# Expert weights of a mixture-of-experts kernel: loads on ScalarE's DMA queue, down pieces split behind the tile loop

## The reference

```python
def _moe_forward(hidden_states, gate_weight, w_gate, w_up, w_down):
    ...
    topk_w, topk_idx = jax.lax.top_k(scores, K)          # K = 8 of E = 64
    topk_w = topk_w / jnp.sum(topk_w, axis=-1, keepdims=True)
    ...
    sorted_tokens = expanded[order]
    group_sizes = jnp.zeros((E,), jnp.int32).at[flat_ids].add(1)
    g = jax.lax.ragged_dot(sorted_tokens, w_gate, group_sizes)
    u = jax.lax.ragged_dot(sorted_tokens, w_up, group_sizes)
    out = jax.lax.ragged_dot(jax.nn.silu(g) * u, w_down, group_sizes)
    ...
    y = jnp.sum(outs * topk_w[:, :, None], axis=1)
x = x + _L0_xattn_ref(_layernorm(x, axis=-1), ctx_2048, ...)
x = x + _L0_ffn_ref(_layernorm(x, axis=-1), ...)
```

## Time and profile before

| | |
|---|---|
| median of 3 runs | 7184.59 us (7184.37 to 7189.35) |
| span of the profiled execution (the page gives its span alone) | 7176.6 us |
| PE busy | 6780.5 us, 94% of the span |
| DVE, ACT, POOL busy | 46%, 42%, 16% |
| experts stage, first gate matmul to last tile's | 3040.19 to 7142.80 us |
| largest part of the chain that ended last, beside PE | DMA 12%, of it `moe_rec_s<-table` 9% |
| bytes moved | 1047.60 MB, mean 146 GB/s |

### The profile page before, as it was taken

The page is one execution under the profiler, slowest core; times in us unless marked ns, Lnnn a source line. Parts: engine busy times, 40 slices in busy tenths (PEclk is TensorE's granted clock), DMA queues, the critical chain, the costliest instruction groups (busy, mean ns, idle before and its releaser), DMA issues.

```text
span 7176.6 us, 104484 instructions
## 1 busy us (share of the span) xinstructions
PE 6780.5 (94%) x34594; PEld 5983.0 (83%) x34595; DVE 3268.1 (46%) x4163; ACT 2987.2 (42%) x3554; POOL 1143.4 (16%) x1037
## 2 busy tenths in 40 slices
PE   8989899999999699699999999999999999999998
PEld 6778787888888577588989888999899999988987
DVE  3433323999999588632343333332322223323333
ACT  3321223888888444333343343332422333333333
POOL 0000000000000145411111111111111111111111
PEclk9999999999999899799999999999999999999999
DMA  7663455555555587555565565554644555555555
GB/s 224 191 199 132 160 137 117 125 130 131 129 125 130 144 159 155 122 146 148 152 199 150 154 174 152 154 152 102 173 103 102 128 129 152 130 148 152 143 144 141
DMA packets 691794, 1047.60 MB, mean 146 GB/s; under 512 B 260259, under 2 KB 489636, under 8 KB 691718
## 3 DMA queue, kind: packets, MB, share of 16 engines
q1 hardware_dynamic: 578916, 672.36, 32.1%
q0 software_dynamic: 112656, 374.28, 23.5%
q10 hardware_dynamic: 146, 0.00, 0.0%
HBM read 724.14 MB, written 322.31 MB: 146 GB/s over the span
## 4 chain that ended last, share of the span: by engine, by line
PE 34%; DMA 12%; ACT 6%; issue 3%; DVE 1%; SPq 1%; ACTq 0%; DVEq 0%; POOLq 0%
DMA moe_rec_s<-table 9%; PE moe_ps_y L1249 4%; PE moe_ps_y L1251 4%; PE moe_ps_y L1250 4%; PE moe_ps_gate L1262 3%; PE moe_ps_gate L1263 3%; PE moe_ps_gate L1264 3%; DMA out<-moe_y,moe_rec_s 3%; PE moe_ps_up L1264 3%; PE moe_ps_up L1262 3%; PE moe_ps_up L1263 3%; ACT moe_gu_hi L1291 2%; ACT moe_d_hi L1291 2%; PE moe_ps_xT L1239 2%; DVE moe_d_lo L1336 1%
## 5 line engine op out<-in xcount | busy, mean ns | idle before, releaser
L1300 ACT ACTIVATE moe_y<-moe_ps_y,moe_rec_s 128x1024 f32<-128x1024 f32 x287 | 320.4, 1116 | 1633.1 <-DMA moe_rec_s<-table 1331.2
L1351 DVE TENSOR_TENSOR moe_hT_lo<-moe_ps_hT,moe_hT_hi 128x384 fp32r<-128x384 f32 x286 | 159.4, 557 | 1637.3 <-ACT moe_hT_hi L1312 1637.3
L1262 PE MATMUL moe_ps_gate<-moe_gu_hi,moe_xT_hi 128*128 128x384 f32 x2288 | 797.7, 349 | 43.1 <-DVE moe_gu_lo L1336 28.0
L1249 PE MATMUL moe_ps_y<-moe_d_hi,moe_hT_hi 128*128 128x512 f32 x1722 | 711.8, 413 | 89.2 <-DVE moe_hT_lo L1351 89.2
L1219 POOL DMA_INDIRECT out<-moe_y,moe_rec_s x287 | 457.7, 1595 | 2083.6 <-ACT moe_y L1300 1987.5
L1263 PE MATMUL moe_ps_gate<-moe_gu_lo,moe_xT_hi 128*128 128x384 f32 x2288 | 772.5, 338 | 0.0
L1264 PE MATMUL moe_ps_gate<-moe_gu_hi,moe_xT_lo 128*128 128x384 f32 x2288 | 772.0, 337 | 0.0
L1264 PE MATMUL moe_ps_up<-moe_gu_hi,moe_xT_lo 128*128 128x384 f32 x2288 | 765.1, 334 | 0.0
L1262 PE MATMUL moe_ps_up<-moe_gu_hi,moe_xT_hi 128*128 128x384 f32 x2288 | 764.2, 334 | 0.0
L1263 PE MATMUL moe_ps_up<-moe_gu_lo,moe_xT_hi 128*128 128x384 f32 x2288 | 764.2, 334 | 0.0
L1251 PE MATMUL moe_ps_y<-moe_d_hi,moe_hT_lo 128*128 128x512 f32 x1722 | 685.9, 398 | 0.0
(11 more groups left out here) (223 smaller groups left out, 14061.0 us busy)
## 6 DMA issues: line engine op xcount, KB each, us to landing
moe_raw_g<-in_w_gate SPq DMA_DIRECT2D x64, 1536.0 KB, 9.0
moe_raw_u<-in_w_up SPq DMA_DIRECT2D x64, 1536.0 KB, 11.0
moe_raw_d<-in_w_down SPq DMA_DIRECT2D x64, 1536.0 KB, 11.5
vst<-proj_v_o SPq DMA_DIRECT2D x64, 512.0 KB, 2.6
att_kt<-kst SPq DMA_DIRECT2D x64, 512.0 KB, 3.5
att_qh<-qst SPq DMA_DIRECT2D x128, 256.0 KB, 4.7
att_ql<-qst SPq DMA_DIRECT2D x128, 256.0 KB, 5.5
att_v<-vst SPq DMA_DIRECT2D x128, 256.0 KB, 3.4
```

The lines of the kernel that those rows point to most:

```text
L1249: nc.tensor.matmul(y_ps[:, cols], hT_hi[:, c], d_hi[:, b, c, cols], start=(c == 0), stop=False)
L1262: nc.tensor.matmul(o[:, 0:I], xT_hi[:, c], gu_hi[:, b, k, c], start=(c == 0), stop=False)
L1300: nc.scalar.activation(y[:], y_ps[:], ACT.Copy, scale=rec_s[:, 1:2]).then_inc(y_done, 1)
```

## The change

The loads of all three weights move from SyncE's program to ScalarE's. Gate and up of expert e + 2 are issued together in ScalarE's first tile of expert e, after its last up piece and after a wait for VectorE's last up piece. The three down pieces of expert e + 1 leave the first tile of expert e, on ScalarE and on VectorE, and are split behind its tile loop; the down load of e + 2 follows there, after a wait for VectorE. For expert 1, all three loads stand behind the split of expert 0. SyncE keeps only its record loads.

```diff
-                def load_weights(e):
-
-                    split_then = (C // 2, C, PIECES)
-                    for k, (raw, src) in enumerate(((raw_g, w_gate), (raw_u, w_up), (raw_d, w_down))):
-                        sp.wait_ge(w_lo_done, PIECES * (e - 1) + split_then[k])
-                        sp.sem_inc(sp_passed, 1)
-                        sp.dma_start(raw[:], src[bass.ds(e, 1)].rearrange("o (c p) i -> p (o c) i", p=P)).then_inc(raw_in[k], 16)
...
                 def expert(e, b, has_next, has_second):
-                    def first(t):
-                        tile(t, isinstance(e, int) and e == 0)
-                        if has_second:
-                            load_weights(e + 2)
-                    expert_tiles(sp, e, first, tile)
+                    expert_tiles(sp, e, lambda t: tile(t, isinstance(e, int) and e == 0), tile)
...
-                def tile(t, e=None, b=None):
+                def load_gate_up(e):
+
+                    act.wait_ge(w_lo_done, PIECES * (e - 1) + GU)
+                    for k, (raw, src) in enumerate(((raw_g, w_gate), (raw_u, w_up))):
+                        act.dma_start(raw[:], src[bass.ds(e, 1)].rearrange("o (c p) i -> p (o c) i", p=P)).then_inc(raw_in[k], 16)
+
+                def load_down(e):
+
+                    act.wait_ge(w_lo_done, PIECES * (e - 1) + PIECES)
+                    act.sem_inc(act_passed, 1)
+                    act.dma_start(raw_d[:], w_down[bass.ds(e, 1)].rearrange("o (c p) i -> p (o c) i", p=P)).then_inc(raw_in[2], 16)
+
+                def tile(t, e=None, b=None, more=False):
...
                     if e is not None:
-                        split(e, b, EARLY, PIECES)
+                        split(e, b, EARLY, GU)
+                    if more:
+                        load_gate_up(e + 1)
...
                 split(0, 0, 0, PIECES)
+                load_gate_up(1)
+                load_down(1)
                 tokens_high(0)
...
                     if has_next:
-                        expert_tiles(act, e, lambda t: tile(t, e + 1, 1 - b), tile)
+                        expert_tiles(act, e, lambda t: tile(t, e + 1, 1 - b, has_second), tile)
+                        split(e + 1, 1 - b, GU, PIECES)
+                        if has_second:
+                            load_down(e + 2)
...
                     if has_next:
                         expert_tiles(dve, e, lambda t: tile(t, e + 1, 1 - b), tile)
+                        split(e + 1, 1 - b, GU, PIECES)
```

More of the change, by code:

```diff
@@ L1107, in experts_pass @@
         dir_in, set_up, ready, pool_passed, sp_passed = s.sem("dir_in"), s.sem("set_up"), s.sem("ready"), s.sem("pool_passed"), s.sem("sp_passed")
+        act_passed = s.sem("act_passed")
         w_hi_done, w_lo_done = s.sem("w_hi_done"), s.sem("w_lo_done")
@@ L1123, in pieces @@
                 yield raw_d[:, c], raw_in[2], d_hi[:, b, c], d_lo[:, b, c]
-        PIECES = C + CI
+        GU = C
+        PIECES = GU + CI
         EARLY = 3
@@ L1172, in _ @@
                     record(rec_g, t + 1, rec_g_in)
-                load_weights(1)
                 def tile(t, is_first=False):
```

## The result

The change takes 7016.55 us (7013.91 to 7019.44) beside 7186.97 us (7184.37 to 7190.32) of the kernel before: a ratio of **0.976**, 95% interval 0.9747 to 0.9772. The forecast was 7016 us.

The account below looks back on a forecast made before the run. PE's own work, 13.66 us a tile, was taken as the floor, with 209.5 us of excess; 41 kept leaves 168.5 gone, so the span 7176.6 becomes 7008.1, plus 8.0 to the median: 7016 us, range 7010 to 7038.

Parts of the forecast that it names:

- The 7.1 us that `y` may be late: Experts stage, ScalarE: `y` may come up to 7.1 us late before PE waits for `hT_lo` at the down matmuls.
- The record beside the loads: SyncE's record load beside 3 MB on another queue: lands in 3 to 5 us, bounds 1.7 and 8.7.
- Down pieces at nothing: Down pieces split behind the tile loop on ScalarE and VectorE: cost nothing, as `hidden` can't run before up is ready.
- Kept: 41 forecast: Part of the 209.5 us excess that stays after the change: 25 + 8.4 + 5 + 2 + 0.6 = 41 us.
- The six waits: PE's waits for next gate weights behind one-tile experts: all six stay, at 4.2 us each, 25 us.
- the clock: PE's slower clock behind a wait: 1.4 us each, six times behind one-tile experts, 8.4 us kept.
- The cold first tile: First tile of the experts stage: keeps some 2 us of excess.
- late records in one-tile experts: Records late beside the down load, and ScalarE's two stands in one tile: 5 us added, bounds 0 and 24.
- The start: Three loads issued ahead of tile 0's `xT_hi`: up to 3.3 us, mostly while PE waits for tokens; 0.6 us taken.
- Rival A: Records don't overtake the weights; 17 experts of one or two tiles lose some 1.8 us each: 7046 us, chance 0.20.
- B: Slower: both records late beside two loads per expert, `y` 9.8 us late, PE pays 4.1 x 57: 7250 us, chance 0.05.
- C: Slower: ScalarE stands at the down load's issue ahead of `silu`, PE loses 4.8 us per expert: 7290 us, chance 0.04.

Follow-up runs that it names:

- the order alone: The change, but SyncE issues all loads, on the records' queue; pieces and loads keep the change's places: 7149.97 us, ratio 0.9974 to the kernel before.
- the down load alone moved: The kernel before, with only SyncE's down load moved behind the tile loop, still on the records' queue: 7053.45 us, ratio 0.984 to the kernel before.
- the run with the pieces back: The change, but all down pieces split in the first tile, ahead of the gate and up loads; down load behind the loop: 7012.86 us, ratio 0.9776 to before.
- the queue alone: The change, but down pieces and their load back in the first tile, loads still on ScalarE's queue: 7199.43 us, ratio 1.0046 to the kernel before.

## Why the prediction was right, and where it was not

**What bounds it.** Right. But for the 3.2 us at the start, the gain is excess over 13.66 us a tile, and the waits for `hT_lo` with what follows them carried most of it. The 7.1 us that `y` may be late hold before the change and with the order alone: no tile with `y` less late waits for `hT_lo`, save the last, and nearly all with more do (56 of 56, and 27 of 31). They are not the whole account. With the down load alone moved, `y` was 7.1 to 10.5 us late in 12 tiles without such a wait, because PE had just stood for `hidden` or at its gate matmuls; the price had only moved.

**The record beside the loads.** I took 3 to 5 us, it took 5.8 in the median, as in the traced expert. The bound, 8.7, held (7.4 the longest), and since 7.1 us are free the difference cost nothing. Right by its place, a little low in size.

**Down pieces at nothing.** Right: one wait for `hidden`, 0.7 us. They needn't have moved at all, though; the run with the pieces back keeps all but 13 us. What had to leave the first tile is the second stand and the down load; the runs don't part these two.

**Kept: 41 forecast, 36.2 in the stage and 3.2 ahead of it.** The six waits are 21.0 us for 25. The tiles in which they fall and those behind them are 33.4 us over 13.66 each, so with 1.1 of smaller waits taken off, 11.3 are left for the clock (granted 0.82 to 0.90 in five of the six tiles behind) where 8.4 was put, 1.9 a wait instead of 1.4. The cold first tile is 1.8 for 2. For late records in one-tile experts 5 was put; what is left is some 2 us, the smaller waits included. The start was put at 0.6 and is 3.2: I priced ScalarE's three issues, but these vanish in its idle time, and what costs is the first gather, which now runs beside the loads and takes 3 us longer. Four terms missed by some 3 to 4 us each, two up and two down, and nearly cancel. That the median came within 1 us of the forecast is luck, where single executions differ by 5.5 us.

**Rival A, the one that failed.** I put the records behind the loads at 7046, since `y` would be "6.1" late, under 7.1. The run with the order alone is that rival nearly to the letter, and it takes 0.9974 of before, 7168 of the first chip's 7187: nearly the whole gain is missing. The step that failed is "some 1.8 us each" in 17 short experts. I let lateness add within one expert and start from nothing in the next; behind experts of up to three tiles the two delays of each, 5.3 and 10.2 us where one was traced, come faster than 3 us a tile pay them off. Had the records not got past the loads, the forecast would have been off by 150 us. By the rule of the Trainium skill (DMA: Bandwidth & Descriptors, "Issuing engines are not separate DMA queues") the queue brings nothing. The trace agrees that the loads still share the engines (the record lands after 5.8 us, not 1.7), and disagrees on what spreading is worth: 153 us of excess between two kernels of one order, most of it where SyncE asks for the record as early in both (19 of the 24 waits behind short experts follow one of two or three tiles).

**Rivals B and C.** B's mechanism, two late records that add up, is what the order alone shows, but on one queue. On two, `y` is at most 4.9 us late. C's mechanism, ScalarE standing ahead of `silu`, is what the queue alone shows; the stand is the wait for VectorE's pieces, though, not the issue, which holds it 0.4 to 0.6 us in the rows shown.

## What to carry to other kernels

A small transfer in a chain that comes round every tile does not belong behind bulk loads on one queue; but the engine that takes over the loads waits for whatever frees their buffers, and that wait must fall where its queue of work has slack, once a tile at most. Measure such a chain against the tile (here 10.8 of 13.66 us): the difference is all that pays lateness off, so add delays over a run of short experts, not over one. And look for the one move that is nearly free first: the down load alone, moved by a few lines on the old queue, brought two thirds.

## What the runs showed of the hardware

- A 1 KB record on a queue of its own, beside 3 MB of loads, landed in 5.8 us (median; the change), alone in 1.7, and behind such loads on their queue in 10.3 (the order alone).
- A 1.5 MB load beside the 512 KB accumulating scatter made the time from the scatter's issue to the next record's 11.0 us instead of 6.97, where the load was issued 0.55 us behind the scatter (the down load alone moved). In the change it is issued some 4 us behind it, and that time stays at 7.1.
- Issuing a load held ScalarE 0.39 us and a second one right behind it 0.57 (0.93 at most in the change), much as on SyncE, and a load was issued while ScalarE's cast ahead of it was still running. I had feared the issue and not the wait ahead of it.
